# Retention layer of a two-layer model: output kept transposed, V weights centred once, gate computed per batch

## The reference

```python
q, k, v, g = x @ w_q + b_q, x @ w_k + b_k, x @ w_v + b_v, x @ w_g + b_g    # 8 heads of 32
q, k = theta_shift(q, sin, cos), theta_shift(k, sin, cos)
sim = einsum('bhnd,bhsd->bhns', q, k / sqrt(32)) * gamma_h ** (n - s)   (0 for s > n)
ret = sim @ v
r = (ret - mean over the 32 of a head) / sqrt(var over the 32 of a head + 1e-5)
y = silu(g) * (r * gn_weight + gn_bias)
x = layernorm(x + y @ w_o + b_o)
```

## Time and profile before

| what | value |
|---|---|
| time, median of 3 runs | 490.53 us (489.29 to 492.24) |
| span of the profiled execution | 489.6 us |
| its mean granted TensorE clock | 0.897 |
| TensorE busy | 405.2 us, 83% of the span |
| VectorE busy | 314.7 us, 64% |
| ScalarE busy | 196.4 us, 40% |
| GpSimd busy | 141.8 us, 29% |

### The profile page before, as it was taken

How to read it: one execution, slowest core, us unless ns; L and a number is a source line. 1 busy time by engine, 2 the same in 40 slices (tenths; PEclk the granted TensorE clock), 3 DMA queues, 4 the chain that set the end, 5 groups by cost and what they waited for, 6 DMA issues and landing times. The chain is left out here.

```text
span 489.6 us, 7799 instructions
## 1 busy us (share of the span) xinstructions
PE 405.2 (83%) x2978; PEld 250.6 (51%) x2978; DVE 314.7 (64%) x689; ACT 196.4 (40%) x356; POOL 141.8 (29%) x182
## 2 busy tenths in 40 slices
PE   2697959568867876888889779998998989999996
PEld 0345646454634542323337334465565757767775
DVE  4547674794877679248438984445646887586554
ACT  4339543123323440588475114635534331241220
POOL 4458874843863000266320001212111000000000
PEclk9879578766989997699899757999999999999999
DMA  7912120200000000005000000000000000000000
GB/s 244 376 28 76 45 55 34 86 0 1 1 1 0 1 2 0 1 11 184 1 0 1 2 0 1 0 3 0 2 2 1 0 1 23 1 0 13 12 12 32
DMA packets 6856, 15.38 MB, mean 31 GB/s; under 512 B 610, under 2 KB 4002, under 8 KB 6818
## 3 DMA queue, kind: packets, MB, share of 16 engines
q1 hardware_dynamic: 6820, 14.89, 9.4%
HBM read 13.84 MB, written 1.05 MB: 30 GB/s over the span
## 5 line engine op out<-in xcount | busy, mean ns | idle before, releaser
L583 PE MATMUL psum_a<-cut_weights,x_transposed 128*128 128x352 f16 (+2 forms) x768 | 141.3, 338 | 12.9 <-DVE cut_weights L1001 8.7
L583 PEld LDWEIGHTS psum_a<-cut_weights,x_transposed 128*128 128x128 f16 x768 | 74.8, 101 | 69.5 <-issue 14.8
L1269 POOL TENSOR_TENSOR ln_rstd<-ln_var_eps,minus_half 128x1 f32<-128x1 f32 x32 | 23.7, 742 | 188.3 <-DVE ln_var_eps L992 188.3
L1286 POOL TENSOR_SCALAR_AFFINE_SELECT arena_mixers<-arena_mixers 128x256 f32<-128x256 f32 (+1 forms) x48 | 24.7, 517 | 108.6 <-ACT arena_mixers L936 108.6
L951 ACT ACTIVATE arena_ffn<-psum_a 128x352 f32<-128x352 f32 x48 | 22.3, 464 | 72.4 <-PE psum_a L583 72.4
L1145 DVE TENSOR_REDUCE arena_mixers<-psum_a 128x2 f16<-128x768 f32 (+3 forms) x44 | 47.3, 1124 | 1.4 <-PE psum_a L740 1.4
L936 ACT ACTIVATE arena_mixers<-psum_a 128x1024 f32<-128x1024 f32 (+2 forms) x48 | 42.0, 883 | 11.1 <-PE psum_a L756 5.7
L1184 DVE SCALAR_TENSOR_TENSOR arena_ffn<-arena_ffn,psum_a 128x352 f32<-128x352 f32 x48 | 24.9, 519 | 31.5 <-ACT arena_ffn L951 16.5
L583 PE MATMUL psum_b<-cut_weights,arena_ffn 128*128 128x256 f16 (+1 forms) x357 | 40.8, 273 | 0.0
L583 PEld LDWEIGHTS psum_b<-cut_weights,arena_ffn 128*128 128x128 f16 (+1 forms) x357 | 34.2, 98 | 5.9 <-issue 1.7
L1187 DVE SCALAR_TENSOR_TENSOR arena_ffn<-arena_ffn,router,psum_a 128x176 f32<-128x176 f32 (+1 forms) x80 | 31.9, 432 | 1.7
(11 more groups left out here) (159 smaller groups left out, 687.0 us busy)
## 6 DMA issues: line engine op xcount, KB each, us to landing
stage<-in_wup SPq DMA_DIRECT2D x8, 512.0 KB, 3.5
stage<-in_wdown SPq DMA_DIRECT2D x4, 512.0 KB, 4.6
arena_ffn<-in_w SPq DMA_DIRECT2D x1, 1408.0 KB, 10.4
stage<-in_xT SPq DMA_DIRECT2D x2, 512.0 KB, 4.4
stage<-in_wqkvg SPq DMA_DIRECT2D x2, 512.0 KB, 5.2
residual<-in_x SPq DMA_DIRECT2D x2, 512.0 KB, 9.1
out<-residual SPq DMA_DIRECT2D x8, 128.0 KB, 1.7
stage<-in_wqkv SPq DMA_DIRECT2D x2, 384.0 KB, 9.9
```

What stands on the lines that cost most here:

```text
L583: ins = mm(dst, lhs[k][a], rhs(k, b, col), start=(k == 0 and a == 0 and b == 0), stop=(bias_at is None and k == n - 1 and a == 1))
L1269: g_.tensor_tensor(rstd[:, r:r + 1], veps[:, r:r + 1], half[:, 0:1], ALU.pow).then_inc(ln_rstd[layer], 1)
L1286: g_.affine_select(out=part, in_=part, compare_op=ALU.is_ge, fill=0.0, base=0, pattern=[[0, se_heads(j)], [1, P]], channel_multiplier=-1). ...
```

## The change

- The columns of w_v and b_v are centred per head before they are cut (new step `cen`, VectorE, on the staged pieces 1 and 2 and on the bias row), so that every head's retention output has mean zero and needs no centring.
- `proj` makes q, k and v only (512 and 256 columns). The gate's input is made per batch, transposed, in the new step `pg`: 12 matmuls of 512 columns; ScalarE adds the bias and takes tanh, VectorE multiplies, once per batch.
- `ret` makes the transposed output: v is the weight (32 columns), the masked scores stream (128 columns), and the four heads of a group write four strips of 32 partitions. ScalarE squares the result and copies it with the norm weight.
- `vr`: TensorE multiplies the squares with a selector of 4 columns, which gives the head variance with tokens on partitions; VectorE adds epsilon, GpSimd takes the power, ScalarE spreads the result over 32 columns per head. `rx`: TensorE transposes that, VectorE multiplies. `yg`: norm bias and gate. `yh`: the cut into head and rest from SBUF. The step `ty` of this layer and `gn` are gone.
- The decay is held in the tables by absolute position, so that the state update is one product with a block mask and one addition.
- `COST` and the needs are rewritten for these steps; `SLACK`, `NUDGE` and `URGE` are not touched. `wo` steps of the two layers are ordered apart. The names of layer 2's `ty` steps become tya and tyb.
- The broadcast of the norm rows (256 KB) becomes a load of a few columns; the constants grow by 48 + 2 columns net of the decay tables and the selector.

The core of the diff:

```diff
-    "kv": "T0.49 D1.77", "ret": "T1.60 A0.30 D0.95 d0.80 p4.40", "gn": "D2.35", "ty": "T0.18 A0.30 D0.40",
+    "cen": "D1.15", "pg": "T2.60 A2.50 d1.20", "proj": "T2.25 A0.90 d0.73 p1.76", "rot": "D1.05", "tqk": "T0.60 A0.50",
+    "sc": "T0.90 A0.50 p0.60", "kv": "T0.49 D0.84", "ret": "T0.90 A1.12", "vr": "T0.40 D0.15 p1.80 a0.38",
+    "rx": "T0.25 D0.42", "yg": "D0.70", "yh": "A0.38 D0.45", "ty": "T0.18 A0.30 D0.40",
...
+        add(("vr", t), ("ret", t), at(t > 1, ("rx", t - 2)))
+        add(("rx", t), ("vr", t), at(t > 1, ("yh", t - 2)))
+        add(("yg", t), ("rx", t), ("pg", b))
+        add(("yh", t), ("yg", t), at(t > 1, ("wo", 0, t - 2)))
+        add(("wo", 0, t), ("yh", t), ("split", 4), at(t > 1, ("ln", 0, t - 2)))
...
-                    ins = cut_product([(ps[:, 0, :], 0), (ps[:, 1, :], 512)], x_tiles(t),
-                                      lambda k, b, c: w[:, b, k, c:c + 512], 0, None if t else weights)
+                    ins = cut_product([(ps[:, 0, :], 0), (ps[:, 1, 0:D], 512)], x_tiles(t),
+                                      lambda k, b, c: w[:, b, k, c:c + (D if c else 512)], 0, None if t else weights)
+                elif kind == "pg":
...
+                    for g in range(KD):
+                        for k in range(KD):
+                            for a, c in ((0, 0), (0, 1), (1, 0)):
+                                ins = mm(ps[:, g, :], w[:, a, k, 3 * D + g * P:3 * D + (g + 1) * P],
+                                         XT[:, c, k, b * TB * P:(b + 1) * TB * P], start=(k == 0 and a == 0 and c == 0),
+                                         stop=(k == KD - 1 and a == 1))
...
-                    for h in range(RH):
-                        g, s = divmod(h, 4)
-                        ins = mm(ps[:, h * RD:(h + 1) * RD], PT[:, t % 2, s // 2, s % 2, g, :],
-                                 VG[:, t % 4, h * RD:(h + 1) * RD],
-                                 start=(h == 0 and not c), stop=(h == RH - 1), skip_group_check=True)
+                    for g in range(2):
+                        for s in range(4):
+                            h = 4 * g + s
+                            ins = mm(ps[32 * s:32 * s + 32, g * P:(g + 1) * P], V0[:, t % 4, h * RD:(h + 1) * RD],
+                                     PT[:, t % 2, s // 2, s % 2, g, :], start=(g == 0 and not c), stop=(g == 1),
+                                     skip_group_check=True)
+                elif kind == "vr":
...
+                    for g in range(2):
+                        ins = mm(ps[:, 4 * g:4 * g + 4], SQ[:, t % 2, g * P:(g + 1) * P], con[:, C_HEAD:C_HEAD + P // RD],
+                                 start=(g == 0), stop=(g == 1), skip_group_check=True)
+                elif kind == "rx":
...
+                        ins = nc.tensor.transpose(ps[:, g * P:(g + 1) * P], SQ[:, t % 2, g * P:(g + 1) * P], ident)
...
+                    nc.scalar.activation(SQ[:, t % 2, :], ps[:, 0:D], ACT.Square)
+                    for g in range(KD):
+                        ins = nc.scalar.activation(RT[:, t % 2, g * P:(g + 1) * P], ps[:, g * P:(g + 1) * P], ACT.Copy,
+                                                   scale=gate_col[:, g:g + 1])
...
-                    link(v.tensor_reduce(sm[:, 0], heads, AX.X, ALU.add))
-                    link(v.tensor_scalar(sm[:, 1], sm[:, 0], -1.0 / RD, None, ALU.mult))
-                    v.tensor_tensor(cent, heads, sm[:, 1].unsqueeze(2).to_broadcast([P, RH, RD]), ALU.add)\
...
-                    link(v.tensor_tensor(SQ, CENT[:, t % 2], CENT[:, t % 2], ALU.mult))
-                    link(v.tensor_reduce(sm[:, 2], SQ.rearrange("p (h d) -> p h d", h=RH), AX.X, ALU.add))
-                    v.tensor_scalar(sm[:, 2], sm[:, 2], 1.0 / RD, EPS, ALU.mult, ALU.add).then_inc(gvar, 1)
...
-                    link(g_.tensor_tensor(GC[:, t % 2], TH[:, t % 2], gate, ALU.mult))
-                    link(g_.tensor_tensor(GC[:, t % 2], GC[:, t % 2], gate, ALU.add))
-                    link(g_.tensor_tensor(GA[:, t % 2], GC[:, t % 2], gnorm[:, 0:D], ALU.mult))
-                    g_.tensor_tensor(GC[:, t % 2], GC[:, t % 2], gnorm[:, D:2 * D], ALU.mult).then_inc(gates, 1)
```

More of the change, by code:

```diff
@@ L129, in dependences @@
     for i, (name, _, _, first) in enumerate(PIECES):
[L131 to L132 removed]
+        if i in (1, 2):
+            add(("cen", i), at(i > 1, ("cen", 1)))
+        add(("split", i), at(i, ("split", i - 1)), at(i in (1, 2), ("cen", i)), at(i > LATE, pv_at(i - LATE - 1) if i - LATE - 1 < 16 else None))
+    add(("bias", 0), ("cen", 2))
     add(("bias", 1), ("bias", 0), ("split", 4))
@@ L137, in dependences @@
     add(("gsum",), ("wsum", 2))
+    for b in range(NB):
+        add(("pg", b), ("split", 3 if b else 2), at(b, ("pg", 0)))
     for t in range(NT):
@@ L212, in name_of @@
     kind = step[0]
-    if kind in ("split", "bias", "wsum", "gsum", "quant"):
+    if kind in ("split", "bias", "wsum", "gsum", "quant", "cen"):
         return kind
-    if kind in ("ty", "wo", "ln", "tx"):
+    if kind in ("wo", "ln", "tx"):
         return kind + str(step[1]) + "ab"[step[2] // TB]
-    return kind + "ab"[step[1] if kind in ("up", "cut", "qk", "tq", "mx", "tm", "se", "pv", "ya") else step[1] // TB]
+    return kind + "ab"[step[1] if kind in ("pg", "up", "cut", "qk", "tq", "mx", "tm", "se", "pv", "ya") else step[1] // TB]
 def schedule():
@@ L255, in schedule @@
                         + [free[times[0][0]]])
-            if step[0] == "split" and step[1] < len(landed):
+            if step[0] in ("split", "cen") and step[1] < len(landed):
                 start = max(start, landed[step[1]])
@@ L664, in _ @@
                     _, layer, t = step
-                    pe.wait_ge(y_rest, NTH[step])
+                    pe.wait_ge(y_rest if layer else y0_rest, NTH[step])
                     if layer == 0 and t == 0:
@@ L1002, in _ @@
                                            ALU.mult, ALU.subtract).then_inc(rest_cut, 1)
+                elif kind == "cen":
+                    i = step[1]
+                    dve.wait_ge(piece_in[i], 16)
+                    parts = [(P, stage[:, i % NSTAGE, 2 * D:3 * D], v_sum[:, i - 1])]
+                    if i == 2:
+                        dve.wait_ge(bias_in, 16)
+                        parts.append((2, bias_raw[0:2, 2 * D:3 * D], v_sum[0:2, 2]))
+                    for _, w, total in parts:
+                        ins = v.tensor_reduce(total, w.rearrange("p (h d) -> p h d", h=RH), AX.X, ALU.add)
+                    link(ins)
+                    for _, w, total in parts:
+                        ins = v.tensor_scalar(total, total, -1.0 / RD, None, ALU.mult)
+                    link(ins)
+                    for rows, w, total in parts:
+                        heads = w.rearrange("p (h d) -> p h d", h=RH)
+                        v.tensor_tensor(heads, heads, total.unsqueeze(2).to_broadcast([rows, RH, RD]), ALU.add)\
+                            .then_inc(v_centred, 1)
                 elif kind == "bias":
```

236 lines of the change are left out of this document (146 added, 90 removed), and 1 row of the table COST.

## The result

The changed kernel takes 507.73 us (median of 4, 506.15 to 508.72) beside 491.24 us for the kernel before (median of 4): ratio 1.0345, interval 1.0302 to 1.0387. It is 16.5 us slower. The forecast was 486.0 us with a range up to 500. Time outside the profiled span is 1.85 us (506.15 against 504.3).

A forecast was written before the change was run, and what follows sets the result against it. Matmul-bound from 331.8 us on; the retention stage before has TensorE idle time and half-speed matmuls behind gaps. Start +3, TensorE -6, y waits -3, second batch -2, order +3.5 make -4.5: 486.0 us from 490.5, range 475 to 500.

The forecast's parts named there:

- TensorE -6: Retention stage: shorter projection and retention products, less added gate and variance products, save about 6 us of TensorE time.
- y waits -3: Retention stage: without gate products queued on GpSimd, TensorE's longest wait for gated output y and its like shrink, 3 us.
- second batch -2: Second batch's retention beside the first's feed-forward: its 8 us share of idle time shrinks by about 2.
- the hand-over behind the retention product: Retention product to output product, per tile: 6.7 us now, 6.3 after, called equal; nothing booked, upper bound +8 us.
- the new order, +3.5: Past 152 us: the planner's recomputed order adds a tenth of 39 us idle; +3.5 booked, bounds -4 and +14.
- The start, +3: Before the first projection: centring delays it, product ends about 3 us later; +3 us, between +1.5 and +4.5.
- The sign given for this step: Past 152 us: TensorE idle time of 39 to 43 us; prediction wrong if above 47 us.
- Rival A: Later stages: order gets worse, a third more of 39 us idle, first feed-forward no earlier; 498 us, chance 0.22.
- the 108 us forecast: First batch's feed-forward, first at 114.2 us, was to start at about 108.
- Rival B: TensorE: two extra waits stall its queue, gaps followed by a stretch at 1.2 GHz; 494 us, chance 0.14.

The follow-up runs named there:

- run 15: Changed kernel in the carried-over order of the kernel before, spread on GpSimd, centring of V weights and bias left out: 491.69 us.
- run 8: Changed kernel with the centring of w_v and b_v left out, order unchanged: 501.37 us.
- run 11: Changed kernel with the order of the kernel before carried over and the spread of the reciprocal deviation on GpSimd instead of ScalarE: 495.50 us.
- 7: Changed kernel with the whole order of the kernel before carried over, each new step in the place of the one it follows from: 504.46 us.
- run 14: Changed kernel, carried-over order, spread on GpSimd, start's centring and splits in turn, new steps placed: 495.09 us.
- run 4: Changed kernel with the order of the kernel before from the end of batch a's row maxima on, earlier part unchanged: 503.65 us.
- run 17: Changed kernel with the spread on GpSimd and the order of the kernel before from the end of batch a's row maxima on: 499.27 us.

## Why the prediction was wrong

Two steps failed. The savings of 11 us (TensorE -6, y waits -3, second batch -2) came to about nothing in a kernel with the order held, because TensorE idles more where it has less to do, and the hand-over behind the retention product, for which nothing was booked, costs 10 us of its waits. And the term for the new order, +3.5, measured +12.2 together with the place of the spread. The terms of the sum, one by one.

**TensorE, -6: right, and the sizes in it partly off.** The retention product takes 0.64 us at full clock instead of the 0.85 booked (16 matmuls), the variance product 0.61 instead of 0.45:

```profile
79.42 0.64 PE L678 MATMUL psum_b<-arena_mixers 128*32 128x128 f32 x16
81.08 0.61 PE L686 MATMUL psum_b<-constants,arena_mixers 128*128 128x4 f32 x4 [1.02 <-ACT arena_mixers L931]
```

That is -9.4 and +4.9 over eight tiles where -7.7 and +3.6 stood. In an order like that of before, the busy time up to the first feed-forward product falls by 6.5 us (run 15). The square and the copy brought no table load: either trace has one, of 1.3 us, at ScalarE's first cut. What failed is that busy time saved would be time saved: 4.1 us of it came back as idle time. (The 0.64 is a row's length, as the 0.43 of the earlier trace rows is; from start to start it is 0.58 in the rows at 113.27 and 113.85 us. The 1.81 is from start to start.)

**The start, +3: inside its bounds with the order held, above them in the planner's.** The first product starts at 10.7 us, as forecast. The second half starts 4.5 us late, since centring of the second piece and of the bias (six VectorE operations from 10.51 to 12.28, then the bias row's cut and the piece's) stands in front of it; that is the upper bound given. In the medians it costs 6.4 us in the planner's order (run 8, whose interval is some 3 us wide to either side) and 3.8 us in the carried one (run 15 against 11).

**The waits for y, -3 and -2 for the second batch: wrong in sign.** This is the step "I book nothing, with +8 as the upper bound" for the hand-over from retention product to output product. The queue of the gate products on GpSimd did go (the power takes 1.69 us in the mean, 1.99 before), and even so TensorE waits for that chain 17.4 us up to 150 us: 12.7 for `y_transposed`, 3.3 at the variance product, 1.4 for the spread; it was 9.8 for y and 4.6 for `y_transposed`, 14.4 us, before. With the order held the same waits are 24.6 us (run 15), 10 us more than before, while the waits for the rotation are 8 us shorter. The lengths alone, 6.7 against 6.3 us by the forecast, do not say this; the chain has ten changes of engine instead of six, and the rows show engines with other work or another wait in front of it (GpSimd at 75.90 us in run 11, ScalarE at 119.77 us in the changed kernel). With the order held, moving one of these changes from ScalarE to GpSimd gave 9.0 us (run 11 against 7), though TensorE's wait for the spread itself did not fall: what fell were waits for other steps' work that ScalarE had held up. The forecast asked whether ScalarE's new work would stand behind other steps, and not what would stand behind its waits. Placing the steps by hand lowered the waits and not the time (run 14).

**The new order, +3.5: the sign right, the size not.** The changed kernel's order costs 12.2 us against the carried order with GpSimd's spread. Of this, 4 us by the medians and 7.6 by the trace lie behind the first `se` product (run 4), the rest in front of it. The sign given for this step, idle time past 152 us of 39 to 43 us and wrong above 47, did show it. From the attention layer's first step to the end, before and after:

```profile
151.80:489.60 337.80, 295.91 (x2368) 0.94 0.04 11
```

```profile
164.70:504.30 339.60, 289.78 (x2316) 0.93 0.04 11
```

TensorE idles 49.8 us there, against 41.9 before (the 39 of the forecast leave out 2.7 us between 300 and 331.8, which the earlier trace rows does not show).

**The rivals.** Rival A (the order gets worse, 498 us; the savings in its sum are 8 us and not the 11 of the forecast, and it does not say why) named a right cause and was held for less likely than the forecast. Its mechanism was another one: it let batch a reach its feed-forward no earlier, and batch a came 10 us earlier, sooner than the 108 us forecast; the time was lost behind that point. Rival B (gaps, and a slow clock behind them) is seen too. Behind the gap of 5.59 us before 147.06 the clock is 0.59, mostly the lower of the two levels:

```profile
147.00:157.00 10.00, 8.99 (x41) 0.59 0.31 97
```

The same output product takes 1.46 us there and 0.83 at 138.90. But up to the first feed-forward product the clock is higher than before (0.82 against 0.78), and up to the first `se` product it is the same (0.83), so B's price was paid in gaps and not in clock. The start and the order alone do not leave the range: at what they measured, 3.8 and 12.2 us (the place of the spread included), the sum gives 495.5. What carries it past 500 is the 11 us of savings that did not come, against which the forecast had only the +8 of the hand-over, as a bound that it did not use.

So the sum as the runs show it: start +3.8 (run 15 against 11); TensorE, y waits and second batch together about 0 (run 15 against the kernel before) instead of -11; order and ScalarE's spread together +12.2 (the changed kernel against run 11) instead of +3.5. That is +16.0, and +16.5 was measured. The terms are differences along one chain of kernels, so that they add up is no proof of them, and another chain would divide the sum otherwise (the start costs 6.4 us if it is taken out of the changed kernel). What stays open is how the 12.2 us divide: the spread alone gives 0.9 us in the planner's order (2.7 by the second median), 4.4 with the later part of the order of before (run 17 against 4) and 9.0 in the carried one, the carried order alone 3.3, so the two act together. Nor is it shown which of the old weights makes the early order bad; only that adding the missing ones changes nothing.

## What to carry to other kernels

Where a greedy planner with hand-set weights gives the order, a change of steps is a change of order of everything: here the weights were worth 65 us to the old steps and 36 to the new. Time the new steps first in the old order, with each new step in the place of the one it follows from, and count the order as a term with its own large bound. And a chain that is cut into more hand-overs between engines can cost more than its lengths add up to (24.6 against 14.4 us of TensorE's waits here, with equal lengths): each engine that waits in its list holds up what stands behind. So look for neighbouring small operations that one engine can do; power and spread on GpSimd gave 9 us in one order and 1 to 3 in another. Price a saving of busy time on a path with waits by the time at which the next stage starts: 6.5 us less work brought 2.4 us here.

## What the runs showed of the hardware

The retention product in the form with 32 weight columns and 128 streamed columns, four strips side by side, takes a row of 0.64 us for 16 fp32 matmuls; with 128 weight columns and 32 streamed the row was 1.97 us. Four times the streamed columns, a third of the time.

A VectorE operation with both inputs in SBUF is not lengthened by every GpSimd operation beside it. In the changed kernel, two stretches of VectorE and GpSimd:

```profile
64.02 1.86 POOL L1354 TENSOR_TENSOR arena_mixers<-arena_mixers,minus_half 128x8 f32<-128x8 f32 x1 [0.79 <-DVE arena_mixers L1139]
64.29 0.42 DVE L1116 TENSOR_TENSOR arena_mixers<-arena_mixers 128x256 f32<-128x256 f32 x1
...
107.44 0.89 POOL L1347 TENSOR_SCALAR_AFFINE_SELECT arena_mixers<-arena_mixers 128x512 f32<-128x512 f32 x1 [3.28 <-ACT arena_mixers L904]
107.75 0.85 DVE L1116 TENSOR_TENSOR arena_mixers<-arena_mixers 128x256 f32<-128x256 f32 x1
```

At 64.29 GpSimd's power of 128x8 has been running since 64.02 (for 1.86 us), and the addition takes its shortest time; at 107.75 GpSimd's mask of 128x512 runs from 107.44 for 0.89 us, and the same addition takes twice as long. The Trainium skill, "SBUF — State Buffer", section "SBUF: two separate sides", describes a port pair that the two engines share under a lock and that the engine which starts first holds for its whole instruction. The second stretch agrees with it; the first does not: this small GpSimd operation did not hold VectorE up for its length. The group's mean is 592 ns with a median of 422, so most of its eight operations ran undisturbed.
